# Long convolution by half-sample transforms with folded halves: one change to a fused two-layer kernel

## Chip, cores and metric

One core of one Trainium2 chip. The metric is device time of one execution in microseconds (us); less is better. "Record" below is one row of the profiler; a matmul in float32 leaves two of them.

## The reference, cut to what matters

Two transformer layers over X of 8 sequences x 256 positions x 256 channels in float32. The change touches the first operator of the first layer alone:

```python
kv = k * v                                   # (8, 256 channels, 256 positions)
kv_f = jnp.fft.rfft(kv, n=512)
kernel_f = jnp.fft.rfft(ssm_kernel, n=512)
y = jnp.fft.irfft(kv_f * kernel_f, n=512)[..., :256]
y = (y + kv * D_skip[None, :, None]) * q
out = einsum('blh,eh->ble', transpose(y), Wo) + bo
```

q and k come from a projection and a three-tap convolution, v from a projection. Behind this operator come a layer norm, an attention layer with a modulated MLP, a second gated operator with a running sum, and a mixture of 64 experts (top 6) with a shared expert; each ends with a residual and a layer norm.

## The kernel before, in words

The five engines run programs of their own and meet at semaphores. The first 660 us or so are ten "turns" of a software pipeline over the 8 sequences; then come the experts (640 to 1000 us) and the final sum.

One turn is written out by hand in `ORDER`, one string of part names for each engine. The first letter says the stage: `A` is the long-convolution operator of sequence b, `Z` its projections for sequence b+1 (at the turn's end, for the next turn), `C` and `u0` to `u15` the attention projections and the 12 attention units of sequence b or b-1, `B` and `f0` to `f7` its MLP, `D` and `S` the second layer's operator, router and shared expert of sequence b-2, `G` and `H` the scattering of rows to the experts by indirect DMA, issued on POOL. Turn 0 ("first") has only A, C and Z; turn 1 ("second") adds attention; turn 2 adds D; turns 3 to 7 also have the twelve scatters `G0` to `G11` on POOL. Turns 8 and 9 have no A part.

An attention unit (`unit`, L857 to L916 on PE) is a loop through four engines: PE scores (L886, L889), DVE maximum (L1587), ACT exponential (L1282), DVE reciprocal of the sum (L1593), POOL scaling (L641), PE transpose (L749), ACT copy out of PSUM (L1275), PE value product (L907, L913). PE scores of unit u wait for the exponential of unit u-2; PE transposes unit u-3 in unit u, and that waits for POOL's scaling.

The parts that the change and the prediction's steps touch:

- `Zk` on DVE (`conv`, L1454 to L1479): convolution of k, then kv = kc * v_sb (L1478), signalled as `a_kv`.
- `Z2`/`A2` on PE (L789 to L801): transposes kv with four PE transposes (L749) into PSUM bank 5; in the first turn, before that, twelve matmuls of the filter's transform (L796). ACT copies the bank to kvT (L1242).
- `A3a`, `A3b` on PE (`forward`, L803 to L814): 4 matmuls each of 128 stationary columns with 256 moving ones, contracting both halves of positions: real parts, then imaginary parts.
- `A3p` on DVE (L1481 to L1498): four products with the filter's spectrum (L1493, 128x512 each); `A3p` on POOL (L621 to L632): difference and sum (L627, L628), then X + bo (L631).
- `A4a`, `A4b` on PE (`inverse`, L816 to L832): for each half of the channels 4 matmuls with 256 moving columns (L824).
- `A4y`, `A4z` on DVE (`gated`, L1520 to L1534): z = y * qc for one half of the channels each (L1527, 128x256).
- `A5` on PE (L834 to L846): projection of z (L744), waits for both halves of z. `A5n`, `A5o` on DVE (L1536 to L1548): residual and moments (vA, L1436), then the scaling; between them POOL's `A5n` takes the root (yA, L649).
- `D1` on PE transposes x (the scaled output of `B8`, DVE L1441), `D2k` on PE projects x2T, which ACT copies behind D1 (L1310). `D3n`, `D3o` are the moments and scaling of the D stage on DVE.
- `again` (L252) lays the experts' buffers over dead tensors, `fwd` and `inv` among them.

Of the kernel before, what the change touches and what calls it, by code (L numbers as in the profile page):

```python
# [28 lines left out]
P = 128  # L29
# [54 lines left out]
def constants():  # L84
# [8 lines left out]
    for k in range(2):  # L93
# [18 lines left out]
    f = np.arange(L)[None, :]  # L112
    w = 2 * np.pi * ((t * f) % NFFT) / NFFT
    re, im = np.cos(w), -np.sin(w)
    sign = 1.0 - 2.0 * (np.arange(L) % 2)
    im_packed = im.copy()
    im_packed[:, 0] = sign
    re_nyq = re[:, :P].copy()
    re_nyq[:, 0] = sign
    fwd = np.concatenate([re, im_packed, im[:, :P], re_nyq], 1)  # L120
    fwd = fwd.reshape(KT, P, 6 * P).transpose(1, 0, 2)
    weight = np.where(np.arange(L) == 0, 1.0, 2.0)[:, None] / NFFT
    ire = weight * re.T
    iim = weight * im.T
    iim[0] = sign / NFFT
    inv = np.concatenate([ire, iim], 0).reshape(2 * FREQ_TILES, P, L).transpose(1, 0, 2)
    return {
        "blank": blank, "cst": c, "csb": b.astype(mybir.dt.np(BF16)),
        "fwd": np.ascontiguousarray(fwd, np.float32), "inv": np.ascontiguousarray(inv, np.float32),
# [3 lines left out]
def build(nc, d):  # L133
# [6 lines left out]
    with ExitStack() as ctx:  # L140
# [18 lines left out]
        fwd, inv = sb("fwd", [P, KT, 6 * P]), sb("inv", [P, 2 * FREQ_TILES, L])  # L159
# [21 lines left out]
        kv, kvT = sb("kv", [P, KT, L]), sb("kvT", [P, TT, D])  # L181
        tabA, tabB, tabD = (sb(n, [P, FREQ_TILES, D]) for n in ("tabA", "tabB", "tabD"))
# [64 lines left out]
        dead = [[t[:].rearrange("p a b -> p (a b)"), 0] for t in (w_in, w_up, w_down, fwd, inv, products.rearrange("p n f d -> p (n f) d"),  # L247
# [11 lines left out]
        def ring(n, *shape):  # L259
# [20 lines left out]
            "ld_vec ld_mlp p_spare n_varA n_varB n_varD n_varR n_invA n_invB n_invD n_invR ld_u ld_uT ld_cst set_skip ld_ak ld_av ld_aq ld_ssm ld_b ld_d set_pool set_dve set_pe set_fold ub "  # L280
            "a_q a_k a_v a_q_out a_k_out a_v_out a_qc a_kc a_kv a_kvT a_kvT_out a_X a_pr a_Y a_y a_z a_o a_r a_x1 "
# [24 lines left out]
        class Chain:  # L306
# [15 lines left out]
            def link(self, ins):  # L322
# [9 lines left out]
                "pool": """""",  # L332
# [17 lines left out]
                "dve": """u0 u1 u2 A3p u3 u4 D2v D2w u5 u6 D3n A4y u7 A4z D3o u8 u9 A5n u10 S0 A5o u11 A6n S1 D4m u12 A6o S2 B6b D4t SD C1 f0 D4k f1 f2 D5p C2 f3 f4 D4w D5h f5  # L350
                        f6 Zk f7 Zq B8""",
                "pool": """G0 u1 u2 G1 A3p u3 u4 G2 G3 G4 u5 u6 G5 D3n u7 G6 u8 G7 G8 A5n u9 u10 G9 G10 u11 A6n u12 C2v G11 D6 C2h B8""",
# [113 lines left out]
        def psum(n, a=0, b=512):  # L466
            return bank[:, n, a:b]
# [16 lines left out]
        def _(sp):  # L484
            sp.dma_start(uT[:], d["uT"][0]).then_inc(S["ld_uT"], 16)
            sp.dma_start(a_w["k"][:], d["a_wk"]).then_inc(S["ld_ak"], 16)
            sp.dma_start(fwd[:], d["fwd"]).then_inc(S["ld_ssm"], 16)
            sp.dma_start(ssm[:], d["ssm"]).then_inc(S["ld_ssm"], 16)
            sp.dma_start(mixed[0:1, :], d["skip"]).then_inc(S["ld_ssm"], 16)
            sp.dma_start(a_w["q"][:], d["a_wq"]).then_inc(S["ld_aq"], 16)  # L490
# [3 lines left out]
            for t, n in ((inv, "inv"), (a_w["o"], "a_wo"), (b_wo, "b_wo"), (b_a, "b_a"), (b_b, "b_b"), *((b_w[n], f"b_w{n}") for n in "qkv")):  # L494
                sp.dma_start(t if n == "b_b" else t[:], d[n]).then_inc(S["ld_b"], 16)
# [113 lines left out]
        def _(pool):  # L609
# [23 lines left out]

            def unit(u):
# [96 lines left out]
        def _(pe):  # L731
# [1292 lines left out]
```

## Time and profile before

| what | value |
|---|---|
| time, median of 3 runs | 1084.31 us (1074.71 to 1090.21) |
| profiled execution, span from first to last instruction | 1034.5 us |
| the median over that span | 49.8 us |
| busy share of the span: PE, PE weight loads, DVE, POOL, ACT | 94%, 77%, 59%, 44%, 33% |
| mean granted TensorE clock | 0.982 |

The page prints a span for the profiled execution and no time of its own. What lies around the span is taken as the difference of the table. In a timeline row the columns are start, length, engine, line, operation, output<-input, shapes, count of merged records, and in brackets the engine's idle time before it with what ended that.

### The profile page before, as it was taken

Reading aid. Unit: us, or ns where it says so; the run is one execution under the profiler, and the core shown is the slowest. Engines: PE = TensorE matmul, PEld = TensorE weight load, DVE = VectorE, ACT = ScalarE, POOL = GpSimd, SP = SyncE. Lnnn points to the kernel's source line nnn. Section 1 sums busy time; section 2 is a strip of 40 time slices with the busy share of each in tenths; the row PEclk is TensorE's granted clock in tenths of the full one; section 3 lists DMA queues with packets and bytes.
Section 4 is the critical chain, followed back from the end, with each engine's and each line's share of the span. In section 5 each row is a group of like instructions: output and inputs, shape, how many; then the busy total and the mean of one; then the engine's idle time right before and its main releaser. Section 6 shows DMA issues by size and latency. Waiting matters only on the chain. (4 is left out here: it accounts for less than half of the span.)

```text
span 1034.5 us, 20988 instructions
## 1 busy us (share of the span) xinstructions
PE 967.6 (94%) x6481; PEld 799.2 (77%) x6481; DVE 608.1 (59%) x2176; ACT 338.7 (33%) x1038; POOL 456.8 (44%) x516
## 2 busy tenths in 40 slices
PE   7988999999999999999999899868999999999986
PEld 6766887877877877877887677647888888888865
DVE  4745466676676676666676546644555555555266
ACT  1244263264264264263263362101111111111243
POOL 1132152283283283283283371541566656656622
PEclk9999999999999999999999999888999999999999
DMA  9597790510510510510510510159869697878296
GB/s 360 192 277 136 203 263 10 133 38 23 137 37 21 137 37 21 137 38 20 128 43 17 129 52 11 64 211 317 335 205 351 211 311 232 295 229 304 85 347 219
DMA packets 103271, 163.28 MB, mean 158 GB/s; under 512 B 26961, under 2 KB 77106, under 8 KB 101042
## 3 DMA queue, kind: packets, MB, share of 16 engines
q1 hardware_dynamic: 85746, 113.31, 37.9%
q0 software_dynamic: 12288, 33.96, 8.7%
q10 hardware_dynamic: 5184, 15.36, 4.1%
q8 instruction: 27, 0.44, 0.2%
q14 instruction: 26, 0.21, 0.1%
HBM read 139.32 MB, written 61.87 MB: 194 GB/s over the span
## 5 line engine op out<-in xcount | busy, mean ns | idle before, releaser
L1282 ACT ACTIVATE prob<-bank,nmx 128x128 f32<-128x128 f32 (+1 forms) x256 | 104.9, 432 | 63.5 <-DVE nmx L1587 63.4
L641 POOL TENSOR_TENSOR prob<-prob,rec 128x512 f32<-128x512 f32 x96 | 99.3, 1041 | 40.8 <-DVE rec L1593 40.0
L673 POOL DMA_INDIRECT x_rows<-x_copy,desti x84 | 85.8, 1021 | 18.3 <-issue 18.3
L1587 DVE TENSOR_REDUCE nmx<-bank 128x2 f32<-128x512 f32 (+1 forms) x96 | 65.1, 685 | 46.6 <-PE bank L889 45.9
L1275 ACT ACTIVATE probT<-bank 128x512 f32<-128x512 f32 x96 | 58.0, 604 | 56.6 <-PE bank L749 55.8
L749 PE MATMUL bank<-cst,prob 128*128 128x128 f32 x384 | 60.6, 282 | 10.3 <-POOL prob L641 6.0
L663 POOL TENSOR_TENSOR products<-z,products 128x512 bf16<-128x512 f32 x8 | 9.2, 1155 | 136.6 <-ACT products L1263 136.6
L949 PE MATMUL bank<-h2T,w_up 128*128 128x256 f32 x256 | 66.4, 382 | 0.0
L951 PE MATMUL bank<-h2T,w_in 128*128 128x256 f32 x256 | 65.7, 379 | 0.0
L749 PEld LDWEIGHTS bank<-cst,prob 128*128 128x128 f32 x384 | 44.4, 145 | 20.2 <-POOL prob L641 10.1
L1282 ACT ACTIVATION_READ_ACCUMULATOR prob<-bank,nmx 128x1 f32 x256 | 55.8, 218 | 0.0
L951 PEld LDWEIGHTS bank<-h2T,w_in 128*128 128x128 f32 x256 | 48.6, 190 | 6.6
L1376 ACT ACTIVATE kc<-bank 128x384 f32<-128x384 f32 x20 | 9.8, 490 | 129.8 <-PE bank L1179 129.8
L1105 PE MATMUL bank<-x3T,sh_gu 128*128 128x256 f32 (+1 forms) x192 | 50.1, 408 | 2.0 <-DVE sact L1820 1.4
L949 PEld LDWEIGHTS bank<-h2T,w_up 128*128 128x128 f32 x256 | 44.9, 190 | 8.6
L962 PE MATMUL bank<-w_down,actT 128*128 128x256 f32 x224 | 49.5, 379 | 0.0
L1304 ACT ACTIVATE gt<-bank 128x256 f32<-128x256 f32 x64 | 24.4, 383 | 74.3 <-PE bank L954 70.1
L1940 DVE COPY d_kv<-bank 128x512 f32<-128x512 f32 x20 | 13.8, 691 | 59.1 <-PE bank L1194 59.1
L1940 DVE COPY d_wq<-bank 128x512 f32<-128x512 f32 x20 | 13.8, 691 | 57.8 <-PE bank L1194 57.8
L962 PEld LDWEIGHTS bank<-w_down,actT 128*128 128x128 f32 x224 | 42.5, 190 | 5.9
L304 POOL TENSOR_TENSOR spare<-ones_row 128x1 f32<-128x1 f32 x49 | 9.3, 189 | 85.4 <-DVE d_cs L1940 52.5
L1376 ACT ACTIVATE x<-bank 128x384 f32<-128x384 f32 x20 | 9.8, 491 | 111.2 <-PE bank L1179 111.2
(445 smaller groups left out, 2500.9 us busy)
## 6 DMA issues: line engine op xcount, KB each, us to landing
w_in<-in_e_w SPq DMA_DIRECT2D x20, 448.0 KB
w_up<-in_e_w SPq DMA_DIRECT2D x20, 448.0 KB
w_down<-in_e_w SPq DMA_DIRECT2D x20, 448.0 KB
products<-in_e_w SPq DMA_DIRECT2D x20, 448.0 KB
prob<-in_e_w SPq DMA_DIRECT2D x20, 448.0 KB
probT<-in_e_w SPq DMA_DIRECT2D x20, 448.0 KB
actT<-in_e_w SPq DMA_DIRECT2D x20, 448.0 KB
x_rows<-sgt SPq DMA_DIRECT2D x1, 8320.0 KB, 28.9
```

Source lines behind the costliest of these rows:

```text
L641: pool.tensor_tensor(p, p, r, ALU.mult).then_inc(S["b_scaled"], 1)
L673: pool.indirect_dma_start(x_rows, bass.IndirectOffsetOnAxis(ap=desti[:, n:n + 1].bitcast(U32), axis=0), rows[:, n // TOPK, :], None).then_ ...
L749: return pe.transpose(out, x, ident)
L949: pe.matmul(psum(n, L, 2 * L), w_up[:, kt, cols], h2T[:, kt, :], start=(kt == 0), stop=(kt == KT - 1))
L951: pe.matmul(psum(n, 0, L), w_in[:, kt, cols], h2T[:, kt, :], start=(kt == 0), stop=False)
L962: mm = pe.matmul(psum(1, tt * D, (tt + 1) * D), actT[:, f, tt * P:(tt + 1) * P], w_down[:, f, :], start=(f == 0), stop=(f == FT - 1))
L1105: mm = pe.matmul(bank[0:w, spread_of(b, n), g * L:(g + 1) * L], sh_gu[:, kt, g * SH_I + at:g * SH_I + at + w], x3T[:, kt, :], start=(kt == ...
L1275: act.activation(probT[:, turned % PROBTS, :, :], bank[:, 2, :].rearrange("p (j q) -> p j q", j=4), ACT.Copy).then_inc(S["b_pT_out"], 1)
L1282: i = act.activation(prob[:, u % PROBS, h * w:(h + 1) * w], psum(u % 2, h * w, (h + 1) * w), ACT.Exp, bias=nmx[:, u, h:h + 1], accum_out=s ...
L1304: act.activation(gt[:, f % 2, :], psum((0, 2, 3)[f % 3], 0, L), ACT.Tanh, scale=0.5).then_inc(S["b_gt"], 1)
L1587: dve.tensor_reduce(nmx[:, u, 0:512 // w], bank[:, u % 2, :].rearrange("p (h k) -> p h k", k=w), AX, ALU.max, negate=True).then_inc(S["b_m ...
L1940: dve.tensor_copy(yc[s], bank[:, to:to + 2, 0:D]).then_inc(S["m_y_out"], 1)
```

## The change

k*v has 256 positions. POOL folds them in a new part `Zf`: position t of the first half plus (and minus) position 255-t of the second half, read backwards. With the time origin at the middle between samples, even frequencies need only the sums and odd ones only the differences for the real part, and the other way round for the imaginary part. So each forward matmul contracts 128 folded values, and 4 matmuls stand where 8 stood. The backward transform makes the even-frequency part and the odd-frequency part of y for 128 positions; each is 128 moving columns wide, and DVE adds and subtracts them to get the first half and the second half (reversed).

```diff
-        fwd, inv = sb("fwd", [P, KT, 6 * P]), sb("inv", [P, 2 * FREQ_TILES, L])
+        long = sb("long", [P, KT, 5 * P])
+        fold, unfold = sb("fold", [P, 4, P]), sb("unfold", [P, 4, P])
+        folded, behind = k_sb[:, :, 2:], kv[:, :, 0:P]
 # ORDER
-                "dve": """... u5 u6 D3n A4y u7 A4z D3o u8 u9 A5n ...          (turn)
+                "dve": """... u5 u6 D3n u7 A4y D3o u8 u9 A5n ...
-                "dve": """A3p u0 u1 u2 u3 u4 u5 A4y A4z u6 ...                (second)
+                "dve": """A3p u0 u1 u2 u3 u4 u5 A4y u6 ...
-                "pool": """... G11 D6 C2h B8"""                               (turn)
+                "pool": """... G11 D6 C2h Zf B8"""
 # SP: fold is loaded behind the filter, unfold where inv stood
+            def Zf(b):                                                        # POOL
+                pool.wait_ge(S["a_kv"], b + 1)
+                need(pool, "a_kvT", b)
+                early, late = kv[:, :, 0:P], kv[:, :, L - 1:P - 1:-1]
+                pool.tensor_tensor(folded[:, :, 0:P], early, late, ALU.add).then_inc(S["a_fold"], 1)
+                pool.tensor_tensor(folded[:, :, P:L], early, late, ALU.subtract).then_inc(S["a_fold"], 1)
 # PE, A2
-                pe.wait_ge(S["a_kv"], b + 1)
+                pe.wait_ge(S["a_fold"], b * 2 + 2)
-                turn_tiles(psum(5), kv).then_inc(S["a_kvT"], 1)
+                turn_tiles(psum(5), folded).then_inc(S["a_kvT"], 1)
 # PE, forward
-                    for n in range(part * FREQ_TILES, (part + 1) * FREQ_TILES):
-                        for kt in range(KT):
-                            mm = pe.matmul(psum(4 + part, (n % 2) * D, (n % 2 + 1) * D), fwd[:, kt, n * P:(n + 1) * P],
-                                           kvT[:, kt, :], start=(kt == 0), stop=(kt == KT - 1))
+                    for n in range(FREQ_TILES):
+                        mm = pe.matmul(psum(4 + part, n * D, (n + 1) * D), fold[:, part * FREQ_TILES + n, :],
+                                       kvT[:, (n + part) % 2, :], start=True, stop=True)
 # PE, inverse(dh)
-                    for n in range(2 * FREQ_TILES):
-                        ...
-                        mm = pe.matmul(psum(4 + dh, 0, L), y[:, n % FREQ_TILES, dh * P:(dh + 1) * P],
-                                       inv[:, n, :], start=(n == 0), stop=(n == 2 * FREQ_TILES - 1))
+                    for i, y in enumerate((Yre, Yim)):
+                        ...
+                        for n in range(FREQ_TILES):
+                            side = (n + i) % 2
+                            mm = pe.matmul(psum(4 + side, dh * P, (dh + 1) * P), y[:, n, dh * P:(dh + 1) * P],
+                                           unfold[:, i * FREQ_TILES + n, :], start=(i == 0), stop=(i == 1))
 # DVE, one A4y where A4y and A4z (gated) were
+            def A4(b):
+                dve.wait_ge(S["a_qc"], b + 1)
+                ...
+                dve.wait_ge(S["a_y"], b * 2 + 2)
+                even, odd = halves_of(4), halves_of(5)
+                dve.tensor_copy(behind, odd).then_inc(S["a_ab"], 1)
+                dve.wait_ge(S["a_ab"], b * 3 + 1)
+                dve.tensor_tensor(odd, even, behind, ALU.subtract).then_inc(S["a_ab"], 1)
+                dve.tensor_tensor(even, even, behind, ALU.add).then_inc(S["a_ab"], 1)
+                dve.wait_ge(S["a_ab"], b * 3 + 3)
+                dve.tensor_tensor(z[:, :, 0:P], even, qc[:, :, 0:P], ALU.mult).then_inc(S["a_z"], 1)
+                dve.tensor_tensor(z[:, :, L - 1:P - 1:-1], odd, qc[:, :, L - 1:P - 1:-1], ALU.mult).then_inc(S["a_z"], 1)
```

ACT's `Z1k`, which writes k_sb, now waits until PE has transposed the folded values of the sequence before. `again` finds other places for the experts' buffers, since the dead tensors have other sizes. The tables loaded at the start are 1152 KB (long 640, fold 256, unfold 256) where they were 1280 KB (fwd 768, inv 512).

## Rows read from the trace of the kernel before

**Rows 1.** The page: part 1, and from part 2 the DMA rate in 40 slices.

```profile
PE 967.6 (94%) x6481; PEld 799.2 (77%) x6481; DVE 608.1 (59%) x2176; ACT 338.7 (33%) x1038; POOL 456.8 (44%) x516
...
GB/s 360 192 277 136 203 263 10 133 38 23 137 37 21 137 37 21 137 38 20 128 43 17 129 52 11 64 211 317 335 205 351 211 311 232 295 229 304 85 347 219
```

**Rows 2.** Timeline of PE, turn 4, from A3a (282 us) to attention unit 11.

```profile
282.30 1.99 PE L811 MATMUL bank<-kvT,fwd 128*128 128x256 f32 x8 [0.38 <-ACT kvT L1242]
...
284.94 0.65 PE L749 MATMUL bank<-cst,x 128*128 128x128 f32 x4 [0.20 <-DVE x L1441]
285.43 1.89 PE L811 MATMUL bank<-kvT,fwd 128*128 128x256 f32 x8
...
287.61 1.99 PE L736 MATMUL bank<-x2T,d_wk 128*128 128x256 f32 x8
...
295.10 1.89 PE L824 MATMUL bank<-inv,products 128*128 128x256 f32 x8
...
297.15 0.60 PE L749 MATMUL bank<-cst,prob 128*128 128x128 f32 x4
...
305.16 1.89 PE L744 MATMUL bank<-a_wo,z 128*128 128x256 f32 x8
...
312.92 0.66 PE L749 MATMUL bank<-cst,prob 128*128 128x128 f32 x4 [1.09 <-POOL prob L641]
```

**Rows 3.** Timeline of POOL, turn 4.

```profile
291.92 1.26 POOL L627 TENSOR_TENSOR products<-products 128x512 f32<-128x512 f32 x1 [0.48 <-DVE products L1493]
...
295.61 2.03 POOL L641 TENSOR_TENSOR prob<-prob,rec 128x512 f32<-128x512 f32 x2
...
311.13 0.72 POOL L649 TENSOR_TENSOR yA<-vA,minus_half 128x2 f32<-128x2 f32 x1
311.83 2.03 POOL L641 TENSOR_TENSOR prob<-prob,rec 128x512 f32<-128x512 f32 x2
```

**Rows 4.** Timelines of DVE (first three) and ACT (last), turn 4.

```profile
284.07 0.73 DVE L1441 TENSOR_SCALAR x<-d_k,mvB,yB 128x256 f32<-128x256 f32 x2 [0.83 <-POOL yB L649]
...
303.36 0.41 DVE L1527 TENSOR_TENSOR z<-bank,qc 128x256 f32<-128x256 f32 x1
...
310.42 0.17 DVE L1436 TENSOR_SCALAR vA<-mvA 128x2 f32<-128x2 f32 x1
```
```profile
286.95 0.61 ACT L1310 ACTIVATE x2T<-bank 128x512 f32<-128x512 f32 x1
```

**Rows 5.** Timelines of PE (first two) and DVE (last), turn 0.

```profile
16.91 3.72 PE L811 MATMUL bank<-kvT,fwd 128*128 128x256 f32 x16 [0.69 <-ACT kvT L1242]
...
27.62 1.05 PE L830 MATMUL bank<-b_a,b_wo 128*128 128x128 f32 x8
```
```profile
31.36 0.70 DVE L1540 TENSOR_TENSOR bank<-bank,X 128x512 f32<-128x512 f32 x1 [0.37 <-PE bank L744]
```

**Rows 6.** kv and what waits for it: DVE at turn 3's end, PE at turn 0's.

```profile
274.36 0.69 DVE L1478 TENSOR_TENSOR kv<-kc,v_sb 128x512 f32<-128x512 f32 x1
```
```profile
52.30 0.65 PE L749 MATMUL bank<-cst,kv 128*128 128x128 f32 x4 [1.02 <-DVE kv L1478]
```

**Rows 7.** Turn 1 on DVE and PE, and turn 2's wait for POOL on PE.

```profile
72.84 0.73 DVE L1527 TENSOR_TENSOR z<-bank,qc 128x256 f32<-128x256 f32 x2
```
```profile
74.25 1.99 PE L744 MATMUL bank<-a_wo,z 128*128 128x256 f32 x8
...
156.66 0.66 PE L749 MATMUL bank<-cst,prob 128*128 128x128 f32 x4 [0.57 <-POOL prob L641]
```

**Rows 8.** POOL and DVE at the same moment of turn 2.

```profile
160.01 1.14 POOL L641 TENSOR_TENSOR prob<-prob,rec 128x512 f32<-128x512 f32 x1 [2.41 <-DVE rec L1593]
```
```profile
160.18 1.26 DVE L1554 SCALAR_TENSOR_TENSOR bank<-X 128x256 f32<-128x256 f32 x1
```

**Rows 9.** Busy times and granted clock by stretches of turn 8 (PE, PEld, DVE, ACT, POOL, PEclk).

```profile
608.00:612.00 4.00, 2.01 (x27) 1.08 (x25) 3.42 (x12) 3.16 (x12) 3.62 (x5) 1.00 0.17 62
612.00:616.00 4.00, 4.00 (x17) 3.45 (x18) 0.76 (x2) 2.29 (x8) 3.77 (x4) 0.57 0.20 72
```

More of the change, by code:

```diff
@@ L111, in constants, with angle, half_angle @@
     t = np.arange(L)[:, None]
[L112 to L126, printed above, removed]
+    even, odd = 2 * p[None, :], 2 * p[None, :] + 1
+    packed = np.where(even == 0, L, even)
+    def angle(f):
+        return 2 * np.pi * ((t * f) % NFFT) / NFFT
+    long = np.concatenate([np.cos(angle(even)), np.cos(angle(odd)), -np.sin(angle(even)), -np.sin(angle(odd)), np.cos(angle(packed))], 1)
+    long[:, 2 * P] = 0
+    long[:, 4 * P + 1:] = long[:, 1:P]
+    long = long.reshape(KT, P, 5 * P).transpose(1, 0, 2)
+    def half_angle(f):
+        return np.pi * (((2 * t[0:P] + 1) * f) % (2 * NFFT)) / NFFT
+    fold = np.stack([np.cos(half_angle(even)), np.cos(half_angle(odd)), -np.sin(half_angle(packed)), -np.sin(half_angle(odd))], 1)
+    weight = np.full((P, 4, 1), 2.0 / NFFT)
+    weight[0, 0], weight[0, 2] = 1.0 / NFFT, 1.0 / NFFT
+    unfold = weight * fold.transpose(2, 1, 0)
     return {
         "blank": blank, "cst": c, "csb": b.astype(mybir.dt.np(BF16)),
-        "fwd": np.ascontiguousarray(fwd, np.float32), "inv": np.ascontiguousarray(inv, np.float32),
+        "long": np.ascontiguousarray(long, np.float32), "fold": np.ascontiguousarray(fold, np.float32),
+        "unfold": np.ascontiguousarray(unfold, np.float32),
     }
@@ L246, in build @@
         cn, cum, pad_e = scr[:, 3], scr[:, 4], scr[:, 5]
-        dead = [[t[:].rearrange("p a b -> p (a b)"), 0] for t in (w_in, w_up, w_down, fwd, inv, products.rearrange("p n f d -> p (n f) d"),
+        dead = [[t[:].rearrange("p a b -> p (a b)"), 0] for t in (w_in, w_up, w_down, long, fold, unfold, products.rearrange("p n f d -> p (n f) d"),
                                                                  prob[:].rearrange("p n (a b) -> p (n a) b", a=4), probT[:].rearrange("p n j q -> p (n j) q"), actT,
@@ L331, in build @@
                 "dve": """Zk""",
[L332 removed]
+                "pool": """Zf""",
             },
@@ L349, in build @@
                 "act": """u0 D1 u1 u2 D2k u3 u4 u5 u6 u7 u8 D4 u9 u10 S0 u11 S1 D4m u12 S2 u13 u14 B6a B6b C1 f0 f1 f2 C2 C2v f3 f4 f5 f6 Z1k f7 Z1v Z1q Z2""",
-                "dve": """u0 u1 u2 A3p u3 u4 D2v D2w u5 u6 D3n A4y u7 A4z D3o u8 u9 A5n u10 S0 A5o u11 A6n S1 D4m u12 A6o S2 B6b D4t SD C1 f0 D4k f1 f2 D5p C2 f3 f4 D4w D5h f5
+                "dve": """u0 u1 u2 A3p u3 u4 D2v D2w u5 u6 D3n u7 A4y D3o u8 u9 A5n u10 S0 A5o u11 A6n S1 D4m u12 A6o S2 B6b D4t SD C1 f0 D4k f1 f2 D5p C2 f3 f4 D4w D5h f5
                         f6 Zk f7 Zq B8""",
-                "pool": """G0 u1 u2 G1 A3p u3 u4 G2 G3 G4 u5 u6 G5 D3n u7 G6 u8 G7 G8 A5n u9 u10 G9 G10 u11 A6n u12 C2v G11 D6 C2h B8""",
+                "pool": """G0 u1 u2 G1 A3p u3 u4 G2 G3 G4 u5 u6 G5 D3n u7 G6 u8 G7 G8 A5n u9 u10 G9 G10 u11 A6n u12 C2v G11 D6 C2h Zf B8""",
             },
@@ L700, in scatter @@
                 return part
-            turns(pool, "pool", {"A3p": A3, "C2v": C2v, "C2h": C2h, "D6": D6, "D3n": inverse_root("D"), "A5n": inverse_root("A"), "A6n": inverse_root("R"),
+            turns(pool, "pool", {"A3p": A3, "Zf": Zf, "C2v": C2v, "C2h": C2h, "D6": D6, "D3n": inverse_root("D"), "A5n": inverse_root("A"), "A6n": inverse_root("R"),
                          "B8": inverse_root("B"), **{f"{g}{n}": scatter(n) for n in range(TT * TOPK) for g in "GH"},
```

45 lines of the change are left out of this document (20 added, 25 removed), and 8 rows, old and new, of the table ORDER.

## The prediction

> **What bounds the kernel now.** I read the page first, then the timelines of the turns, engine by engine, asking at each A part which engine is late there. The page says PE: 94% busy, DVE 59%, POOL 44% [rows 1]. If that share told the whole story, every matmul taken away would shorten the run. It is a mean over stages, and an engine that waits 1 us five times a turn still shows as nearly full. So the question is what PE meets behind each place where it gets faster. The parts of A lie in turns 0 to 7, and five of these (3 to 7) are alike; turn 4 stands for them.
>
> In turn 4 three waits pin PE between 282 and 313 us.
> First, D1 transposes x at 284.94 after a wait of 0.20 us for DVE [rows 2]; DVE finishes x at 284.80, and that chain began at the end of the last MLP matmuls, which the change does not touch [rows 4].
> Second, the scores of unit 2 need the exponential of unit 0, behind which ACT starts x2T at 286.95, and D2k needs x2T, which ends at 287.56; D2k starts at 287.61 [rows 2, 4]. PE was not early there by more than 0.1 us.
> Third, POOL. It starts the spectrum's difference at 291.92 after a short wait for DVE; from there to 313.86, when it ends the scaling of units 8 and 9, its timeline shows no wait for anybody, only work and the 0.2 to 0.3 us before each scatter [rows 3]. PE transposes unit 2 at 297.15, 0.5 us after POOL scaled it (two in 2.03 us from 295.61), and it waits 1.09 us for unit 8 at 312.92 [rows 2, 3]. There are five such waits of about 1.1 us, one for each turn from 3 to 7. POOL fills these 22 us of the turn, PE runs beside it with about 1 us to spare. What makes POOL start earlier would pay; what makes PE faster before 312.92 doesn't. Behind 312.92 PE is the bound until the MLP ends, and nothing is removed there.
>
> **The change, part by part.**
> Forward matmuls. Sixteen records of 256 moving columns fill 3.72 us less the 0.27 us in which the last one drains, so 0.216 us a record and 0.43 us a matmul [rows 5]. Four of eight go: 1.73 us a turn, half in A3a, half in A3b.
> Backward matmuls. Eight stay, with 128 columns instead of 256. The price of such a float32 matmul is in turn 0: eight records in 1.05 us, less a last one that overlaps by 0.16: 0.11 us a record, 0.22 us a matmul [rows 5]. Eight times 0.21 is 1.67 us a turn. Together 3.4 us of PE a turn, 27 us over 8 turns: this is the most that the change can give.
> The fold, `Zf` on POOL. No row has this operation with 256 elements. Two inputs of 128x512 from SBUF take 1.26 us, and so little work as 128x2 takes 0.72 in a power [rows 3]; I take 0.7 us each, 1.4 together, and keep 0.6 and 2.5 as bounds for the pair, the upper one if reading backwards costs as much as twice the elements. In a steady turn kv is ready at 275.05 [rows 6] and PE transposes it after B8's matmuls, at 280.9, just ahead of A3a at 282.30 [rows 2]: 5.8 us of cover, for which even 2.5 is little. POOL has nothing else there. Without that cover, at the end of turn 0, PE already waits 1.02 us for kv [rows 6], and the 1.4 us come on top.
> The rest of Z. Z1k's new wait is for transposes that lie a whole turn back: nothing. Loads: 128 KB less ahead of the filter's tables, 0.4 us at the first slice's 360 GB/s [rows 1]; fold arrives behind them, before kvT is ready.
> The unfolding on DVE. Before: two products of 0.41 us [rows 4], 0.73 for two in a row [rows 7]. After: copy, subtract, add, two products, each of 256 elements a partition, with three semaphore waits between. At the price of the product and 0.33 us from start to start, with 0.05 to 0.1 us for each wait, the part takes 2.0 us, 1.25 more than before. From below an operation might cost 0.33, from above 0.7 as for 512 elements (the residual add, 0.70 [rows 5]): 1.7 to 3.6 us for the part. It can also start only when both halves of the channels are done.
> What is queued behind it: the scaling of D3o, the maximum of u8 and u9, then A5n, whose moments POOL takes up. On PE, A5 waits for z.
>
> **The sum, turn by turn.**
> Turn 0: nothing else runs. A3 ends 1.7 us earlier and the tables 0.4 earlier; the products on DVE follow, so A4y starts 2.1 us earlier and ends 0.8 us earlier than A4z did plus what A5's filler work covers. DVE then has to split B before A5n, which starts 2.0 us earlier, at 29.4 where it was 31.36 [rows 5]. To the next transposes of kv: -2.0 + 1.4 for Zf. Then A3a and A3b in one go, -1.7: attention starts 2.3 us earlier.
> Turn 1: A4a and A4b stand together, -1.67; scores and transposes of u5 and u6 lie before A5. DVE does u5 at 70.5, the unfolding to 73.2, and A5 starts at 73.25 where it was 74.25 [rows 7]: 1.0 us gained.
> Turn 2: no scatters, but the same x, x2T and X + bo chain, so A3 gives nothing and A4a 0.4. The unfolding now ends after PE has done u8; A5 starts 0.4 us later than before, the moments of A come 0.4 us later, POOL takes units 8 and 9 behind them, and PE already waits 0.57 us for unit 8 [rows 7]: 0.4 us lost.
> Turns 3 to 7: D1 waits 1.1 us instead of 0.2, so A3a's 0.86 is gone; unit 2's scores and D2k wait for ACT, so A3b's 0.86 is gone. A4a's 0.84 leaves 0.45 before POOL's unit 2. Half a microsecond early, DVE is through D3n and u7 at 303.45, unfolds until 305.45; A5 starts at 305.5 (it was 305.16 [rows 2]), and vA is there at 311.1 where it was 310.59 [rows 4]. POOL takes it at 311.13 [rows 3]: just in time. PE's unit 8 comes at 312.9 as before. Gain 0, five times.
> Experts: other addresses, same work: 0.
> Total: -2.3 - 1.0 + 0.4 = -2.9 us. The profiled execution spans 1034.5 us, so a span of 1031.6 is expected, and with the 49.8 us that lie between span and median, 1081.4 us. The three runs reach from 1074.7 to 1090.2, so one median of such runs can be off by 7 us; a change below about 2% (22 us) can't be told from none here.
>
> One rule of the Trainium skill speaks against Zf. At 160.18 a DVE operation with two inputs from SBUF takes 1.26 us where its twin just before took 0.41, while POOL scales beside it until 161.15 [rows 8]. SBUF — State Buffer (SBUF: two separate sides) says that such a DVE instruction and a GpSimd one that reads SBUF exclude each other for the whole instruction, and the rows agree. By that, Zf (two inputs from SBUF) may hold up qc's convolution on DVE or be held by it: at most the 2.5 us of that convolution, hidden in a steady turn, and in turn 0 the gain there would be 2.5 us smaller. The five unfolding operations have one input in PSUM each and are free of it.
>
> **Rivals.**
> (a) PE is the bound all through. For it speak its 94% [rows 1] and that the POOL waits are only 1.1 us. Against it: the waits named above, which stand ahead of all that gets faster. Time: all 27 us, less the 1.4 of Zf: 1059 us. Perfetto Trace Analysis of the Trainium skill (Identifying the Most-Contended Engine) has one optimise the engine with the highest occupancy, while it calls matmul busy time a poor measure for TensorE; by the first half this rival would hold.
> (b) The unfolding becomes the bound, and the kernel is slower than before. Place: DVE between u7 and A5n. If an operation costs 0.7 us, the part takes 3.6, 1.6 more than I count. It decides as soon as vA comes after 311.13, and nothing is left of that margin: then every further 1 us delays POOL's units 8 and 9 and with them PE at 312.92. Turns 1 to 7, seven times 1.4 us, is +10, with the -3 from above +7: 1091 us. Against it: rows of DVE with one input in PSUM show 0.41 us for 256 elements throughout [rows 4].
> (c) The clock. With the new waits PE stands still for 2.1 us between 284 and 287.6. In turn 8 a stretch of 4 us with PE busy for 2.0 has the clock at 1.00, and the next one has 0.57 [rows 9], near 1.2 instead of 2.4 GHz for most of it, which costs 1.7 us. If that happens in each of turns 2 to 7: +10 us, of which the slack before 312.92 absorbs most. Without the slack: 1091 us; with it 1083.
> (d) The POOL chain moves earlier because something in DVE's or ACT's order is freed that I took for fixed: 1 us a turn, 1075 us.
>
> **How the numbers follow.** My forecast 0.66; (a) 0.06; (b) 0.12; (c) with its full price 0.08; (d) 0.08. The forecast with (c) absorbed and the noise of a median reaches from 1074 to 1089. To leave no more than 2 in 10 out, the range takes in (b), (c) and (d): 1067 to 1095. Faster by over 2% (below 1062.6) is (a) alone: 0.06. Slower by over 2% (above 1106) needs (b) and (c) together and bad runs: 0.02. Same: 0.92.
>
> **What would show it.** Right: PE busy falls by about 27 us while the span stays within a few us; forward records halve to 64; the wait of PE for x before D1 grows to about 1.1 us; the wait for unit 8 on POOL remains 1 us or grows to 3 (PE's gain A4b ends there); the turns keep their 77.5 us; A5 waits for z. Wrong: turns of 75 us or less would mean that POOL was not the bound; vA after 311.5 in turn-4 terms and turns of 79 us mean (b); windows with a clock near 0.6 inside turns 3 to 7 mean (c).

## The result and the profile after

The change makes the kernel slightly slower: 1089.08 us (median of 20 runs, 1080.66 to 1100.38) against 1082.69 us for the kernel before (20 runs, in the same set), a ratio of 1.0062 with a 95% interval of 1.0036 to 1.0087, so 6.4 us, some 4 to 9. A second comparison in another set of runs gives 1.0053 (1.0028 to 1.0078). Forecast were 2.9 us less. Ratios and their intervals, here and below, leave out runs that took over 1.5% more than the fastest of the same kernel, among them three of the 20 after the change, three of the ten of no_unfold (1230 to 2405 us) and one of the four of early (1904 us). The profiled execution has a span of 1088.4 us in a run of 1090.2.

From the page of the kernel after, part 1 and the clock in 40 slices:

```profile
PE 973.9 (89%) x6417; PEld 793.6 (73%) x6417; DVE 627.2 (58%) x2200; ACT 340.1 (31%) x1038; POOL 467.6 (43%) x532
...
PEclk9988999999999999999999999788989989899999
```

PE has 64 records fewer, as the change says, yet its busy sum is no smaller than in [rows 1]. That sum holds the experts' stage too, which is some 40 us longer here for a reason that is not the change (last section). The second profile of the kernel after has the faster experts' stage, like that of [rows 1], and there the sum is 949.2 us, 18 less. The matmuls that were changed have rows of their own. Groups of instructions by line, before (two rows) and after (two rows): count, busy us, mean ns, and the idle time before them:

```profile
L811 PE MATMUL bank<-kvT,fwd 128*128 128x256 f32 x128 | 30.8, 386 | 3.4 <-ACT kvT L1242 3.4
L824 PE MATMUL bank<-inv,products 128*128 128x256 f32 x128 | 30.7, 385 | 1.7 <-DVE products L1497 1.7
```
```profile
L826 PE MATMUL bank<-kvT,fold 128*128 128x256 f32 x64 | 18.3, 417 | 3.4 <-ACT kvT L1258 3.4
L840 PE MATMUL bank<-unfold,products 128*128 128x128 f32 x128 | 18.4, 292 | 1.7 <-DVE products L1513 1.7
```

61.5 us became 36.7: the 27 us foretold are 24.8. PE really got that time; it then waits. PE's waits (us in total, times, longest), before and after:

```profile
PE bank L749 <- POOL prob L641: 6.0, 6, 1.1
...
PE bank L749 <- DVE x L1441: 2.4, 5, 1.6
...
PE bank L1105 <- DVE sact L1820: 1.4, 2, 0.8
```
```profile
PE bank L758 <- DVE z L1549: 10.4, 8, 1.5
...
PE bank L1121 <- DVE sact L1841: 7.5, 6, 1.5
PE bank L763 <- DVE x L1457: 7.0, 7, 1.1
...
PE bank L763 <- POOL prob L655: 6.2, 15, 0.7
```

z and x were foretold. The line that was not is the third kind: PE's `S2` (L1121, the shared expert's third part) waits 1.3 to 1.5 us a turn for `sact`, which before it did in two places only. (sact is the shared expert's activation, a product on DVE, L1841 and before the change L1820; S0, S1 and S2 are its three parts.)

**How long the turns are.** ACT's copy to kvT starts once a turn, so its starts measure turns. Between two profiled executions of the kernel before they differ by 0.6 us at most. The times are us; the last column is the mean of turns 3 to 6.

| kernel | kvT of sequence 0, 1, 2, 3 | of sequence 7 | a turn |
|---|---|---|---|
| before | 16.3, 53.0, 126.1, 204.1 | 514.3 | 77.55 |
| before, second profile | 16.3, 53.0, 126.2, 203.5 | 513.9 | 77.6 |
| after | 15.4, 51.7, 127.3, 204.6 | 524.4 | 79.95 |
| after, second profile | 15.9, 52.7, 125.0, 202.3 | 522.1 | 79.95 |

Three of these four turns take 79.5 us after the change and one takes 81.2. The steady turns are the loss; turns 0 to 2 together end between 1.8 us earlier and 1.1 us later than before (kvT 3 at 202.3 and 204.6, against 203.5 and 204.1).

**Inside a steady turn.** Turn 5 of the kernel after starts 83.7 us behind turn 4 of before (kvT at 365.4 and 281.7); subtract that to compare with [rows 2 to 4]. PE:

```profile
368.66 0.65 PE L763 MATMUL bank<-cst,x 128*128 128x128 f32 x4 [1.07 <-DVE x L1457]
...
370.80 0.39 PE L902 MATMUL bank<-csb 128*128 128x512 bf16 x1 [0.62 <-ACT prob L1298]
...
389.75 1.99 PE L758 MATMUL bank<-a_wo,z 128*128 128x256 f32 x8 [1.46 <-DVE z L1549]
...
397.14 0.66 PE L763 MATMUL bank<-cst,prob 128*128 128x128 f32 x4 [0.66 <-POOL prob L655]
...
403.09 1.97 PE L1121 MATMUL bank<-x3T,sh_gu 128*96 128x256 f32 x8 [1.29 <-DVE sact L1841]
```

D1 starts at 284.96 in the terms of turn 4 (284.94 in [rows 2]), as foretold. A5 starts at 306.05 (305.16 there, 305.5 foretold), unit 8 is transposed at 313.44 (312.92), S2 starts at 319.39 (317.45 before). So 0.5 us are lost by unit 8 and another 1.4 between unit 8 and S2, where the forecast had looked at nothing. S2 had no slack there before either: it started 0.05 us behind the sact that it needs. DVE and PE of the kernel before, turn 4:

```profile
316.98 0.42 DVE L1820 SCALAR_TENSOR_TENSOR sact<-sgs,bank 128x256 f32<-128x256 f32 x1
```
```profile
317.45 1.97 PE L1105 MATMUL bank<-x3T,sh_gu 128*96 128x256 f32 x8
```

DVE and POOL of the kernel after in the same turn 5:

```profile
386.36 0.76 DVE L1452 TENSOR_SCALAR vD<-mvD 128x2 f32<-128x2 f32 x1
387.04 0.68 DVE L1608 TENSOR_REDUCE nmx<-bank 128x2 f32<-128x512 f32 x1
...
387.71 0.39 DVE L1543 COPY kv<-bank 128x256 f32<-128x256 f32 x1
388.14 0.43 DVE L1545 TENSOR_TENSOR bank<-bank,kv 128x256 f32<-128x256 f32 x1
...
389.28 0.41 DVE L1549 TENSOR_TENSOR z<-bank,qc 128x256 f32<-128x256 f32 x1
...
395.10 0.17 DVE L1452 TENSOR_SCALAR vA<-mvA 128x2 f32<-128x2 f32 x1
...
400.29 1.68 DVE L1575 SCALAR_TENSOR_TENSOR bank<-X 128x256 f32 x1
```
```profile
385.04 2.04 POOL L655 TENSOR_TENSOR prob<-prob,rec 128x512 f32<-128x512 f32 x2
...
395.36 0.72 POOL L663 TENSOR_TENSOR yA<-vA,minus_half 128x2 f32<-128x2 f32 x1 [0.54 <-issue]
...
400.62 1.05 POOL L655 TENSOR_TENSOR prob<-prob,rec 128x512 f32<-128x512 f32 x1
```

Two of DVE's operations end with a POOL operation instead of by their own length. vD, 128x2 elements, takes 0.76 us and ends at 387.12, when POOL's two scalings end (387.08). The second product of A6n (L1575, two inputs from SBUF; L1554 before) takes 1.68 us and ends 0.3 us behind the scaling of unit 10 (401.67). Its twin in turn 5 of before had taken 0.49:

```profile
392.91 0.49 DVE L1554 SCALAR_TENSOR_TENSOR bank<-X 128x256 f32 x1
```
```profile
393.92 1.05 POOL L641 TENSOR_TENSOR prob<-prob,rec 128x512 f32<-128x512 f32 x1
```

There POOL's scaling started 1.01 us behind the product's start, when the product was over; here 0.33 us behind it. Behind the product, DVE computes sact for PE's S2.

### The profile page after: what moved, and what is told of

It is laid out like the page before. It is cut to its first block and busy times, and to the rows that moved or that the text cites. A ratio compares the mean times of both kernels' runs of the same rounds, so it can differ in the third digit from the quotient of the medians.

```text
span 1088.4 us, 20920 instructions
## 1 busy us (share of the span) xinstructions
PE 973.9 (89%) x6417; PEld 793.6 (73%) x6417; DVE 627.2 (58%) x2200; ACT 340.1 (31%) x1038; POOL 467.6 (43%) x532
## 5 line engine op out<-in xcount | busy, mean ns | idle before, releaser
L1298 ACT ACTIVATE prob<-bank,nmx 128x128 f32<-128x128 f32 (+1 forms) x256 | 104.7, 430 | 72.9 <-DVE nmx L1608 72.3
L1121 PE MATMUL bank<-x3T,sh_gu 128*128 128x256 f32 (+1 forms) x192 | 49.6, 405 | 8.1 <-DVE sact L1841 7.5
L1961 DVE COPY d_wv<-bank 128x512 f32<-128x512 f32 x20 | 13.8, 691 | 60.9 <-PE bank L1210 44.5
L1392 ACT ACTIVATE d_kv<-bank 128x384 f32<-128x384 f32 x20 | 9.8, 490 | 122.4 <-PE bank L1195 76.4
L1121 PEld LDWEIGHTS bank<-x3T,sh_gu 128*128 128x128 f32 (+1 forms) x192 | 35.2, 193 | 17.4 <-DVE sact L1841 11.4
L1320 ACT ACTIVATE gt<-bank 128x256 f32<-128x256 f32 x64 | 24.4, 383 | 73.2 <-PE bank L970 71.5
```

The source lines that it names most:

```text
L1121: mm = pe.matmul(bank[0:w, spread_of(b, n), g * L:(g + 1) * L], sh_gu[:, kt, g * SH_I + at:g * SH_I + at + w], x3T[:, kt, :], start=(kt == ...
L1298: i = act.activation(prob[:, u % PROBS, h * w:(h + 1) * w], psum(u % 2, h * w, (h + 1) * w), ACT.Exp, bias=nmx[:, u, h:h + 1], accum_out=s ...
```

## The experiments

**Theory:** POOL bounds the turn up to unit 8, as foretold, so the 24.8 us of PE are worth nothing; the loss is the unfolding, which makes z late, and then the meeting of A6n's product with POOL's scaling. **Rivals:** the loss is the fold or the folded matmuls themselves; or the clock; or the other places of the experts' buffers.

The kernels ran in four sets, each with runs of the kernel before; in these it took 1084.5 us (set 1), 1037.2 (2), 1037.9 (3) and 1090.1 (4). Only ratios inside a set are compared. A turn, as above, is the mean of turns 3 to 6; where the text names another length, it is that of most of them.

| kernel | set, ratio to before (95%) | kvT 1, 2, 3 | kvT 7 | a turn |
|---|---|---|---|---|
| no_unfold | 1, 0.9949 (0.9910 to 0.9988) | 50.6, 119.4, 196.6 | 509.6 | 78.25 |
| before_three | 1, 1.0112 (1.0070 to 1.0153) | 53.4, 126.9, 205.0 | 523.6 | 79.65 |
| early | 1, 0.9889 (0.9815 to 0.9963) | 53.1, 126.0, 202.7 | 513.1 | 77.6 |
| layout | 2, 0.9999 (0.9981 to 1.0017) | 52.5, 127.7, 205.7 | 515.9 | 77.55 |
| root_first | 2, 0.9992 (0.9969 to 1.0015) | 53.1, 125.7, 202.8 | 516.7 | 78.5 |
| filled | 2, 1.0065 (1.0037 to 1.0094) | 52.2, 126.6, 204.0 | 523.9 | 80.0 |
| early_x | 2, 0.9905 (0.9875 to 0.9936) | 53.1, 125.9, 204.7 | 511.1 | 76.6 |
| after_again | 3, 1.0053 (1.0028 to 1.0078) | 52.7, 125.0, 202.3 | 522.1 | 79.95 |
| early_again | 3, 0.9951 (0.9934 to 0.9968) | 52.7, 124.9, 201.5 | 511.8 | 77.6 |
| before_x | 3, 1.0038 (1.0016 to 1.0060) | 52.8, 127.9, 205.2 | 520.9 | 78.9 |
| both_out | 3, 0.9922 (0.9892 to 0.9952) | 50.8, 124.4, 202.8 | 513.1 | 77.6 |
| before_x_root | 4, 0.9990 (0.9948 to 1.0033) | 52.7, 127.9, 205.1 | 516.5 | 77.85 |
| early_x_root | 4, 0.9970 (0.9931 to 1.0010) | 52.9, 125.3, 203.7 | 515.0 | 77.8 |

**Is the unfolding the loss?** no_unfold is the kernel after without the copy, the subtraction and the addition (they are left out of the computation).

```diff
-                dve.tensor_copy(behind, odd).then_inc(S["a_ab"], 1)
-                dve.wait_ge(S["a_ab"], b * 3 + 1)
-                dve.tensor_tensor(odd, even, behind, ALU.subtract).then_inc(S["a_ab"], 1)
-                dve.tensor_tensor(even, even, behind, ALU.add).then_inc(S["a_ab"], 1)
-                dve.wait_ge(S["a_ab"], b * 3 + 3)
```

> The changed kernel without the copy, the subtraction and the addition of the unfolding (left out of the computation). Theory: the unfolding's 1.2 us on DVE are what delays A5, the moments of A and all behind them. Then turns 3 to 6 take 77.5 us as before, the wait of PE for z before A5 is at most 0.3 us, and the last kvT copy starts at about 511 us (524.4 with the change). Rival, Zf on POOL and the shorter matmuls with their waits are the cause: turns stay at 79.5 us or more. Time against before: 1 to 3 us less by the theory, 5 more by the rival.

before_three puts the same three operations (their results unused) into DVE's A4z of the kernel before, ahead of its product.

```diff
+                    if eh == 1:
+                        dve.tensor_copy(kv[:, :, 0:P], odd).then_inc(S["a_ab"], 1)
+                        ...
+                        dve.tensor_tensor(kv[:, :, P:L], even, kv[:, :, 0:P], ALU.subtract).then_inc(S["a_ab"], 1)
+                        dve.tensor_tensor(kv[:, :, 0:P], even, kv[:, :, 0:P], ALU.add).then_inc(S["a_ab"], 1)
```

> The kernel before with three DVE operations of 256 elements added ahead of the second product of z (a copy, a subtraction, an addition, results unused). Theory: they alone lengthen turns 3 to 7 by nearly 2 us each, the last kvT copy starts at 522 to 525 us (514.3 before), 1% slower. Rival (the changed matmuls or Zf are needed for the loss): under 0.5 us a turn, below 517 us.

Both came out close. Three operations of 0.42 us each cost the kernel before 1.1% and the same turns as the change; without them the change gains 0.5% (no_unfold has the 6417 PE records of the kernel after, so the experts' work is as much, though the values are others). And no_unfold bears out the bound that the forecast was built on. In its turn 4 (kvT at 274.9, so 6.8 us ahead of before's) PE has 3.1 us less of matmuls, and transposes unit 8 where before did, 31.2 us into the turn, after the same wait (1.09 us in [rows 2]):

```profile
306.12 0.66 PE L763 MATMUL bank<-cst,prob 128*128 128x128 f32 x4 [1.09 <-POOL prob L655]
...
311.34 1.97 PE L1121 MATMUL bank<-x3T,sh_gu 128*96 128x256 f32 x8 [0.79 <-DVE sact L1836]
```

The second row keeps the turn at 78.25 us and not at the 77.5 expected; a wait of S2 for sact is there although A6n's product takes 0.47. What comes late in it is the tanh of S1's output on ACT, which DVE needs for sact: in turn 6 it starts 0.72 us behind the last record of S1's matmuls, where before it started 0.04 us behind (table below). Why was not found.

**Is the place of the unfolding all?** early is the kernel after with both backward halves together on PE and the unfolding ahead of unit 6 on DVE.

```diff
-                "pe":  "... D2q A4a u5 D3 u6 A4b u7 u8 A5 ..."
+                "pe":  "... D2q A4a A4b u5 D3 u6 u7 u8 A5 ..."
-                "dve": "... D2w u5 u6 D3n u7 A4y D3o ..."
+                "dve": "... D2w u5 A4y u6 D3n u7 D3o ..."
```

> The changed kernel with A4b moved up beside A4a on PE and the unfolding put before unit 6 on DVE, where DVE stood still for 2.7 us. Theory (place, not size of the unfolding): A5 does not wait for z any more, turns take 77.5 us or a little less, the last kvT copy starts at 509 to 512 us, time 1 to 4 us under before. Rival (size): 79 us a turn whatever the place, since POOL and DVE share what they need.

> The early order once more, beside before. Theory (its turns are as long as before's, and only turns 0 to 2 are 1.2 us shorter): last kvT at 513, 0 to 3 us faster than before. Rival (the 12 us of the first measurement are real): 8 us or more faster.

The turns are back at 77.6 us, PE doesn't wait for z from turn 2 on, and the kernel is faster than both before and after: 5 us by the second, larger measurement (the first has three runs), whose interval, 3.3 to 6.9 us, leaves out the rival's 8 us and the theory's 0 to 3 as well. It is more than the 2 us that the turns gained; where the rest comes from was not found.

**Is it DVE and POOL?** root_first changes only POOL's order in the kernel after: A6n's root, which can't start before the product on DVE is through, goes ahead of unit 10's scaling.

```diff
-                "pool": "... A5n u9 u10 G9 G10 u11 A6n u12 ..."
+                "pool": "... A5n u9 u10 G9 G10 A6n u11 u12 ..."
```

> After the change, with POOL taking the root of A6n before the scaling of unit 10. Theory (A6n's second product on DVE takes 1.68 us instead of 0.46 since POOL's scaling runs beside it, and the router's activation comes late by it): that product is back at 0.46 us, PE's wait for sact before S2 falls from 1.3 us to under 0.8, turns of 78 to 78.5 us instead of 79.5, last kvT at 516 to 520 instead of 524, 4 to 7 us faster than after. Rival (A6n is late because z is late, the lock adds nothing that ends on PE): product 0.46 but turns of 79.5, last kvT 523 to 526.

DVE and POOL of root_first, turn 4:

```profile
316.02 0.46 DVE L1575 SCALAR_TENSOR_TENSOR bank<-X 128x256 f32 x1
```
```profile
316.82 0.72 POOL L663 TENSOR_TENSOR yR<-vR,minus_half 128x2 f32<-128x2 f32 x1 [0.25 <-DVE vR L1579]
317.53 2.08 POOL L655 TENSOR_TENSOR prob<-prob,rec 128x512 f32<-128x512 f32 x2
```

The product is back at 0.46, the waits for sact fall from 7.5 us to 2.5, a turn is 1.0 us shorter, and no turn has the long 81 us: the kernel equals before. The theory's window held on each count. Up to the product this kernel and the second profile of after run within 0.04 us of each other (table below), so the 1.0 to 1.1 us is what the collision costs here. A turn still takes 0.9 us more than before without it: that part is z's lateness.

both_out does this and what no_unfold did (the same part of the computation left out).

> After the change, without copy, subtract and add (left out of the computation, as in no_unfold), and with A6n's root ahead of unit 10's scaling on POOL (as in root_first). Theory (the 2.0 us that a turn loses are 1.25 us of unfolding in DVE's way, which make z late, and 1 us of A6n's product beside POOL, and nothing else): turns of 77.2 to 77.6 us, last kvT at 503 to 507. Rival (something else that the change brought, such as Zf or the folded matmuls, holds the turn): 78 us or more, last kvT as no_unfold's, 508 to 511.

The turns are the 77.6 us of before: with the unfolding and the collision both gone, nothing of the loss is left. So fold and folded matmuls cost a steady turn nothing. kvT 7 lies 6 us beyond the foretold window, since turns 1 and 2 were 6 us longer than in no_unfold (74 and 78 us against 69 and 77), turn 1 with a clock of 0.68 between 85 and 90 us.

**Does it pay to relieve POOL, which bounds the turn?** before_x moves X + bo (1.26 us on POOL) in the kernel before from A3p to the end of the turn before; early_x does the same to early.

```diff
             def A3(b):
-                pool.tensor_tensor(slots(X, b), slots(X, b), bo[:]...broadcast_to([P, TT, D]), ALU.add).then_inc(S["ub"], 1)
+            def Zf(b):     # last on POOL but B8; in early_x behind the fold
+                pool.tensor_tensor(slots(X, b), slots(X, b), bo[:]...broadcast_to([P, TT, D]), ALU.add).then_inc(S["ub"], 1)
```

> The kernel before with X + bo alone moved on POOL, from A3p to the end of the turn before. Theory (POOL bounds the turns of before from A3p to unit 8, and PE has about 1 us of slack there): turns of 76.5 to 77 us instead of 77.5, last kvT at 508 to 511 instead of 514, 3 to 6 us faster than before. Rival (PE is the bound of before, which has 3.4 us more of matmuls a turn): turns of 77.5, last kvT 513 to 515.

> The early order (both backward halves together, unfolding before unit 6's maximum), and X + bo moved from POOL's A3p to POOL's Zf, a turn earlier. Theory (POOL is the bound from A3p to unit 8, 22 us of each turn): 1.26 us of it go, PE's wait for unit 8 falls from 1.1 to under 0.5 and the wait for unit 4 too, turns of 76.3 to 77 us where early has 77.6, last kvT at 505 to 509 instead of 513, 4 to 8 us faster than early. Rival (PE's other waits, x, the exponential and z, hold the turn): turns of 77.4 or more, last kvT 512 or later.

early_x had the turns foretold (76.6), but not the rest: the wait for unit 8 stayed at 1.1 us, since PE came earlier too, and the last kvT start is 511.1 instead of 505 to 509, since turn 2 took 78.9 us (76.7 in early). before_x went against theory and rival: with 1.26 us less ahead of it, it is slower by 0.4% and its turns take 78.55 us (one 80.1). POOL and DVE of before_x, turn 4:

```profile
314.33 0.72 POOL L650 TENSOR_TENSOR yA<-vA,minus_half 128x2 f32<-128x2 f32 x1 [0.41 <-DVE vA L1437]
...
319.58 1.06 POOL L642 TENSOR_TENSOR prob<-prob,rec 128x512 f32<-128x512 f32 x1
```
```profile
319.01 1.93 DVE L1555 SCALAR_TENSOR_TENSOR bank<-X 128x256 f32 x1
```

This is the collision of the kernel after, without any part of the change. The product starts 4.93 us behind vA (in [rows 4] vA is at 310.42, the product at 315.35), and the scaling of unit 10 about 5.25 behind yA. Where POOL waits for vA, yA follows it by 0.25 us and the two meet, every turn. Where POOL takes yA up 0.7 us late, as in [rows 3, 4], or 1.1 late, as in early_x (vA at 308.74, yA at 309.81), they miss. early_x, turn 5:

```profile
390.26 0.46 DVE L1574 SCALAR_TENSOR_TENSOR bank<-X 128x256 f32 x1
```
```profile
391.63 1.05 POOL L654 TENSOR_TENSOR prob<-prob,rec 128x512 f32<-128x512 f32 x1
```

before_x_root and early_x_root add root_first's order to these two.

> before_x (X + bo earlier on POOL, which made turns of 78.55 us) with A6n's root ahead of unit 10's scaling on POOL. Theory (before_x was slower because POOL, no longer late at vA, starts that scaling 0.57 us behind the start of A6n's second product on DVE and holds it up; with the order changed that can't happen): the product takes 0.46 us instead of 1.93, PE's waits for sact before S2 fall from 7.1 to under 3 us in all, turns of 76.5 to 77.6 us, last kvT at 509 to 515 instead of 521. Rival (POOL's lateness is worth something else, such as the order of scaling and transposes): turns of 78 us or more, last kvT 518 or later.

> early_x with the same change of order on POOL. Theory (there POOL takes up vA about 1 us late as in before, so its scaling starts 1.4 us behind the product and the two never meet; the change can only delay unit 10's scaling): turns of 76.6 to 77.2 us, last kvT at 511 to 514, within 3 us of early_x. Rival (A6n's root is on the path, and earlier is better): last kvT 509 or less and 2 us or more faster.

In before_x the product is back at 0.46 us and a turn at 77.85, 0.7 us shorter: right in kind, 0.25 us beyond the theory's window for the turn, the kvT start and the total wait for sact (4.4 us against under 3) likewise. In early_x, where the two don't meet, the same order makes a turn 1.2 us longer, a little more than foretold. So the order has a price too, and it pays only where it avoids a collision: 1.0 us a turn in root_first, 0.7 in before_x_root. The two ratios of set 4 are too wide to say more than this.

**All of it in one turn.** Turn 6 has no clock fall in any of these kernels. Times are us behind the kernel's own start of kvT; the column on tanh has the end of S1's last matmul record and the start of the tanh of S1's output on ACT (where it starts 0.4 us behind that end, ACT is still at unit 11's exponentials).

| kernel | A5 starts | unit 8 transposed | A6n's product takes | S1 ends, tanh starts | sact ends, S2 starts | turn |
|---|---|---|---|---|---|---|
| before | 23.46 | 31.22 | 0.47 | 34.37, 34.41 | 35.69, 35.75 | 77.56 |
| after_again | 24.37 | 31.77 | 1.93 | 34.92, 35.29 | 37.66, 37.71 | 79.52 |
| root_first | 24.36 | 31.76 | 0.47 | 34.91, 35.28 | 36.57, 36.63 | 78.43 |
| no_unfold | 23.12 | 31.21 | 0.46 | 34.36, 35.08 | 36.37, 36.43 | 78.23 |
| both_out | 23.11 | 31.21 | 0.46 | 34.36, 34.40 | 35.69, 35.75 | 77.55 |
| before_x | 23.46 | 30.76 | 1.92 | 33.91, 34.28 | 36.64, 36.69 | 78.50 |
| before_x_root | 23.46 | 30.76 | 0.46 | 34.26, 34.68 | 35.97, 36.03 | 77.83 |
| early_x | 21.89 | 30.23 | 0.47 | 33.38, 33.43 | 34.72, 34.77 | 76.58 |
| early_x_root | 22.19 | 30.72 | 0.46 | 33.87, 34.66 | 35.95, 36.01 | 77.81 |

In every row the turn is S2's start plus 41.8 us, so whatever delays S2 is lost in full. After the change two things delay it: A5, which is 0.9 us late behind z, and the collision, 1.1 us here (after_again against root_first). A third has nothing to do with the product's length: in no_unfold and early_x_root tanh starts 0.7 and 0.8 us behind S1's records, and changing POOL's order takes this away in one case (both_out) and brings it in the other. Its cause is open, and so POOL's order has more effects on S2 than the collision alone. The 1.9 us between before_x and early_x are not the collision's price: A5 also starts 1.6 us earlier in early_x.

**The clock and the buffers.** filled puts three idle matmuls ahead of A5's wait in every turn. layout gives `again` in the kernel before pieces as long as those after the change.

```diff
-                if first(b):
-                    idle(2, 7)
+                idle(2 if first(b) else 3, 7)
```
```diff
+        cut = [fwd ... [:, 0:5 * KT * P], inv[:, 0:2, :] ..., inv[:, 2:4, :] ...]
```

> After the change, with three idle matmuls of PE's warm-up kind ahead of A5's wait for z in every turn. Theory (PE's wait of 1.5 us before A5 lets the clock fall in turns 1 and 4): A5 of turn 4 takes 2.0 us instead of 3.5, the window 90 to 95 us has a clock near 1.0 instead of 0.62, last kvT at 518 to 521 instead of 524. Rival (the clock falls of other causes, and the fill delays A5 where it runs over the wait): last kvT 524 to 528.

> The kernel before, with the dead tensors given to the placing of the experts' buffers in pieces as long as those after the change (1280, 512 and 512 columns where 1536 and 1024 stood): the turns can't change, last kvT start 514 as before. Theory (the turns lost 10 to 12 us by the profiles and the time only 6, because the experts' buffers lie better): 4 to 8 us faster than before. Rival (the placing is worth nothing, and the difference is what the experts' stage varies by between executions): within 2 us of before.

> The kernel after the change once more, beside the kernel before. Theory (the loss is in turns 3 to 7, which take 79.5 us instead of 77.5, and in a fall of the clock at 90 to 95 us, and the same in every execution): last kvT start at 523 to 525 us and 9 to 12 us slower than before. Rival (part of it is the phase of the turns against the clock, and varies): last kvT start below 522, 4 to 8 us slower.

filled did nothing: the wait for z shrank to 0.16 us, yet a long turn is still there (81.2 us, turn 5, clock 0.63 from 400 to 404 us), and the clock still falls at 85 to 95 us. layout comes out at 0.9999: other addresses for the experts' buffers cost and gain nothing beyond its interval of 2 us either way, and the theory that they make up for part of the turns is dead. after_again lies between the two on kvT, 522.1 against the theory's 523 to 525 and the rival's under 522, and has the rival's time (5.5 us). At the last scaling of x_row, in turn 8, the two profiles of after are 10.8 and 8.7 us behind before's first; what takes 3 to 4 us of that back in the time of both measurements, behind 620 us, stays open.

Clock falls do add to the loss. The kernel after, stretches with their busy times (PE, PEld, DVE, ACT, POOL) and granted clock (third from the right), and A5 of turn 4:

```profile
85.00:90.00 5.00, 2.84 (x28) 1.89 (x32) 1.46 (x3) 2.52 (x7) 2.01 (x2) 0.70 1.48 82
90.00:95.00 5.00, 5.00 (x30) 3.85 (x27) 0.73 (x2) 1.42 (x4) 0.00 (x0) 0.62 0.02 6
308.00:312.00 4.00, 3.45 (x9) 2.69 (x10) 2.06 (x6) 1.07 (x5) 3.56 (x4) 0.61 0.09 34
```
```profile
308.55 3.49 PE L758 MATMUL bank<-a_wo,z 128*128 128x256 f32 x8 [1.46 <-DVE z L1549]
```

At A5 eight records take 3.49 us instead of 1.99, near 1.2 instead of 2.4 GHz, and turn 4 is 81.2 us. The fall at 90 to 95 us costs turn 1 about 3 us (75.6 us, against 72.3 in after's second profile with the clock at 1.00). But the kernel before has the fall at 85 to 90 us too, layout has it at 90 to 95 us (0.50), root_first and early not at all. So the change alone does not bring it; what does is open.

## Why the prediction was wrong

By its parts:

- PE's gain, 27 us on paper: 24.8, and off the path of the steady turns as argued. Rival (a) is excluded by both_out: 3.1 us less of matmuls a turn, and turns of 77.6 us.
- Fold: 0.74 us each (16 rows, 5.9 us for each eight), foretold 0.7; covered in steady turns. In turn 0 it costs more than its own time: kv's product starts at 48.73, POOL's two operations end at 50.96, and PE waits 2.41 us for them where it had waited 1.02. The qc operation beside them took 1.52 us where its kc twin took 0.74, so the exclusion foretold for this place came, at DVE's cost, though on the operation ahead of the convolution that was named.
- Turn 0: A5n's addition started at 28.70 us, foretold 29.4; the gain was then lost behind it (36.3 and 36.8 us from kvT 0 to kvT 1, where before took 36.7). Foretold were 2.3 us, got 0.3 to 1.3, most of it from the earlier start (kvT 0 at 15.4 and 15.9), and layout, whose turns are those of before, starts at 15.8 too. Turn 1: foretold -1.0, got -0.9 (72.3 us, the clock up) and +2.4 (75.6, the clock down). That is no clean comparison, since before's 73.2 has a clock fall of its own, and layout took 75.2. Turn 2: foretold +0.4, got -0.6 against before's first profile and 0 against its second.
- The unfolding: foretold 2.0 us at 0.41 an operation, got 1.98 (387.71 to 389.69). The price that rival (b) feared was not the trouble.
- **The step that failed: "Turns 3 to 7", gain 0 five times, on the sum "DVE is through D3n and u7 at 303.45, unfolds until 305.45", "vA is there at 311.1", "just in time".** It failed twice. First, PE's half microsecond of lead never reached DVE: vD in turn 4 of before already took 0.48 us and ended with POOL's scaling (303.44, POOL 303.40), and after the change it starts 0.3 us earlier and ends at the same moment. So u7 ends at 304.0 instead of 303.45, the unfolding at 305.99, A5 starts at 306.05 instead of 305.5, and vA ends at 311.57. That is 0.44 us past the 311.13 named as the point of decision, and unit 8 came 0.5 us later, as by rival (b)'s mechanism. That the hold on vD, which ends with POOL's scaling in either kernel, is what kept the lead from DVE is read from these rows; no run took it away alone. Second, the sum ended at unit 8 with "behind 312.92 PE is the bound". But S2 followed sact by 0.05 us before, so DVE had no slack there: A5's 0.9 us reach S2 in full (root_first), and A6n's product, which POOL's scaling had missed by half a microsecond, now meets it and adds 1.0 to 1.1 us. S2 waits 1.3 us for sact, and a steady turn loses 1.9 us. Five turns of that are 9.5 us, against 0 foretold.

So rival (b), to which 0.12 was given, had the sign, the place and nearly the time (1091 us), and its sign in the profile, turns of 79 us, is what the trace shows. It had the wrong price: the operations took 0.4 us and not 0.7, and half of the loss is the collision, which no rival named for this place. Rival (c) was partly right: one clock fall in turns 3 to 7 and not one in each. The span around which the forecast was built was also read wrongly. The 49.8 us between span and median are not "around the span"; every other profile's span lies 1.8 to 1.9 us under its own run. The first execution was one with a fast experts' stage, of the kind of sets 2 and 3.

The rule of SBUF — State Buffer (SBUF: two separate sides) in the Trainium skill, which the prediction weighed for Zf alone, names the operation that decided: one of DVE with two inputs from SBUF, against one of GpSimd that reads SBUF (it also names DVE operations in a 2-port mode; whether vD is one no run shows). The traces agree on the whole-instruction wait (1.68 and 1.93 us for 0.46). The page lets the one that "starts first" go first, and the records' starts don't bear that out: POOL's scaling, whose record starts 0.33 to 0.58 us behind the product's, runs its plain 1.05 us, and the product ends 0.3 us behind it. Either the rule is off here or a record's start is not the moment that counts; the runs can't tell. In the kernel before, with 1.01 us between the starts, the two did not overlap at all.

## What to carry to other kernels

On a path of several engines, end the sum not where the first late part is absorbed but where the order of the next operations is restored: look at how much slack the next engine has (S2 had 0.05 us), at what runs beside each DVE operation with two SBUF inputs, and by how much it misses POOL now. A bound engine that is relieved can make the kernel slower (before_x), since its lateness had kept two operations apart (the product took 1.93 us there and 0.46 with POOL's order changed); and a DVE part that is added should go where DVE is idle and POOL isn't waiting for what is behind it (early), which turned 0.5% of loss into 0.5% of gain.

## What was not expected of the hardware

The experts' stage has two speeds, for both kernels alike. The kernel before was profiled once more in set 1 to see how far profiles repeat.

> The kernel before, unchanged, profiled a second time. The first profile spans 1034.5 us though no timed run of it was under 1070. If the ten turns of the pipeline are the same in every execution and the experts' stage is what varies, the last copy to kvT starts at 514 us again and the span is about 1080. If the turns vary as well, that copy starts at another time.

The turns repeat; the experts don't. Waits of PE in the second profile of the kernel before; the first has none of this kind:

```profile
PE bank L1179 <- issue: 11.1, 13, 1.1
...
PE bank L1190 <- issue: 3.2, 5, 1.0
```

Behind the last scaling of x_row (near 611 us in both) the run takes 423 us in the one profile and 462 in the other. Busy times and clock of 680 to 1000 us, first profile and second:

```profile
680.00:1000.00 320.00, 307.39 (x2394) 262.71 (x2394) 158.70 (x709) 51.22 (x123) 172.28 (x212) 0.97 0.78 267
```
```profile
680.00:1000.00 320.00, 289.67 (x2218) 242.03 (x2218) 141.92 (x647) 38.38 (x81) 156.20 (x191) 0.93 0.73 242
```

7% fewer matmul records in the same time, with gaps in which PE waits for nothing that the profile shows. The cause is open. Sets 2 and 4 ran on the same chip and have either speed (1037.2 and 1090.1 us), so the chip alone does not decide it. It moves the time by 50 us, eight times what the change does, so a single profile's span must not be set against another set's median.
